# Two one-column values of each attention tile made on ScalarE instead of VectorE, expert loads issued one by one, and every slot rewritten

## The chip, the core and the metric

The kernel runs on one core of a Trainium2 chip. The metric is the device time of one execution in microseconds. A core has five engines that matter here: TensorE (PE in the profile, its weight loads PEld), VectorE (DVE), ScalarE (ACT), GpSimd (POOL) and SyncE (SP), which issues most of the loads and stores. Each engine takes its instructions in the order in which they are written; across engines, semaphores hold an instruction back until another one is done.

## What is computed

The input is 8 batches of 512 rows of 256 values, with a context of 1024 rows of 192 values for each batch. A layer normalisation, then a cross attention that keeps the 32 largest scores of each row, then a convolution over time done as a Fourier transform, a feed-forward layer, and at last a mixture of eight experts, of which each row goes to one, beside a shared one:

```python
Q = (x_text @ Wq).reshape(Bb, Tt, H, DH)                      # 4 heads of 32
scores = jnp.einsum('bthd,bghd->bhtg', Q, K) / np.sqrt(DH)
topv, topi = jax.lax.top_k(scores, K_TOP)                     # 32 of 1024
probs = jax.nn.softmax(topv, axis=-1)
attn = zeros.at[..., topi].set(probs); attn_mean = attn.mean(axis=1)
c_t = jnp.einsum('btg,bgd->btd', attn_mean, V)
# c_t scales and shifts the rows ahead of and behind the convolution s4d
x = x + jnp.tanh(g_xattn) * layernorm(xt + gelu(layernorm(xt) @ W1 + b1) @ W2 + b2)
x = x + jnp.tanh(g_ffn) * (shared(h) + expert[argmax(h @ gate_w)](h * score))
```

The same operation as before and after the change is asked for: the softmax over the 32 kept scores of each row and head.

## The kernel before

**Tiles and batches.** Attention works in 128 tiles, 16 to a batch: four groups of 128 rows, four heads each. Tile n's scores (128 x 1024) are made by TensorE in two of four PSUM banks (L1967, L1968). VectorE then finds the 32 largest of each row in four rounds: a maximum of eight (L1491 from PSUM, L1499 from SBUF) and a replacement that strikes these eight out (L1495, L1503), the replacement only after the first three rounds. ScalarE makes the exponential of all scores from PSUM, the sum of exponentials of the 32 kept ones, a ramp that tells kept scores from others (L1117), the logarithm of the reciprocal sum, and with it the exponential that turns the ramp into 0 or the reciprocal sum. GpSimd multiplies that by the exponentials and adds up the four heads (L776, L778, L780). TensorE turns the sum and multiplies it with the context (L1986, L1995).

**Two small values.** Each tile needs minus its scaled maximum, as the bias of the exponentials, and the reciprocal of its sum. Before, VectorE makes both in `limits()` (L1511 and L1514), counted by one semaphore, `v_limit`. The first must come behind the tile's first maximum, the second behind ScalarE's sum. ScalarE's `attention()` waits for the first ahead of its exponential of all scores and for the second ahead of the logarithm. Columns 0 to 3 of the tile's small buffer `sm` hold minus the scaled maximum, the sum, the reciprocal and its logarithm; there are three of these buffers, two each of `ee` and `tk`, the wide ones. A replacement of tile n writes `tk[n % 2]`, which GpSimd's product of tile n - 2 must have read.

**Behind attention.** For each batch: forward transform (L2211), spectrum, inverse transform (L2223), normalisations (moments, an ScalarE root, a GpSimd correction), a feed-forward layer with Gelu (L2247, L2257), the router, the shared expert (L2312, L2321). Rows are scattered to regions of DRAM by expert. From the fourth batch on 21 full tiles of 128 rows of one expert are worked off between the other work (`tiles()`, L2331 to L2351), each with its rows (L679) and its expert's weights (L684, L689) loaded by SP. In the last stage all eight experts' weights are loaded into the space that attention has left (`expert()`, L693 to L697), and the 18 remaining tiles run in a loop (L2370, L2380).

**What sets the order.** Every engine has a list of generators, one for each kind of work, that yield a number ahead of each piece: its slot. `weave` takes the piece with the smallest slot, then that generator's next, so a piece whose slot is smaller than what has gone before follows at once, and the numbers only set an order. Tile n's slots are counted from 8n. The tables of slots stand at the head of the file. `keep_warm` lets TensorE multiply a constant (L1945) a given number of times ahead of a piece; the FILL tables give the counts. ScalarE's functions come in tables; a change of table is an instruction of its own.

**SP's queue.** `late()` loads the inverse transform's table and the second weight of the feed-forward layer (L616, L617), `keys()` moves a batch's keys into place (L640, L642), `post()` reads x a second time (L662) and stores four result blocks (L667), `routed()` loads the experts.

Of the kernel before, what the change touches and what calls it, by code (L numbers as in the profile page):

```python
# [14 lines left out]
ALU = mybir.AluOpType  # L15
# [111 lines left out]
def tile_slot(j, table, step=0):  # L127
# [14 lines left out]
POOL_RESIDUAL = ((130.1, -4.1, -719.1, -97.8), (-203.7, 134.9, -261.3, -103.3))
POOL_OUT = ((-4044.4, -1439.6, -1614.3, -1706.4), (-1035.6, -458.3, -104, -271.7))
POOL_ROUTE = ((132.7, -16.2, -361.3), (135.4, 143.2, 144.9))
POOL_SH = ((238.9, -304.4, 243, 166.5), (152.6, 8.2, -1104.8, -2520.3))
POOL_PREP = (74, 75)
POOL_LOW = (105.1, 75.4, 76.7)
ACT_FILM_IN = ((43.7, -264, -187.1, -62.9), (-23.2, -497.2, 31.1, -313.4))
ACT_INV = ((69.3, -21.2), (48.4, -137.9))
ACT_FILM_OUT = ((72.4, -176, -155.8, -229), (51.5, -210.2, -467.8, 61.9))  # L150
ACT_ROOT = ((75.3, -138.8, 139.6), (71, -4004.6, 95.2))
ACT_NORM = ((84.6, 143.1), (-574.9, 50.3))
ACT_TURN = ((89.8, -324.7), (-4056.4, -177.3))
ACT_UP = ((99, 87.7, -389.9, 83.9, -76.5, -267.9, 106.2, -123.2), (-24, 84.5, -1154.9, -1053.5, 0.4, -343.5, -15.1, -1046.2))
ACT_DOWN = ((116.6, -45.3, -83, 121.2), (13.1, -263.3, 107.4, -198.8))
ACT_OUT = ((129.9, -538.2, 43.2, -140), (59.2, -943.2, -1370.1, -755.4))
ACT_TURN2 = ((147.5, -1744.3), (109.2, -588.1))
ACT_ROUTE = ((-3375.8, 83.1), (-1449.5, 127.6))
ACT_SILU = ((118.7, 155), (91.5, 140.1))
ACT_SH = ((166.5, -331.8, 168.6, 91), (145, -206.6, -505.3, -552.7))  # L160
DVE_SPECTRUM = ((115.4, -156.1, 116.8, -505.8), (54.3, -166.3, -118.6, -647.3))
DVE_MOMENTS = ((137.1, 171.7), (-368.7, 86.3))
DVE_ROUTE = ((177, 181.9), (51.2, -62))
ACT_PREP = (30, 35.9, -1091.9)
ACT_QUERY = (44.4, 21.7, 50.3)
ACT_CONTEXT = (26.7, 72)
ACT_KEY = (38.4, 74)
ACT_FINISH = ((20.6, -514.7, 28, 42), (34.8, 23.8, 43.8, 50), (29.1, -233.8, 44.8, 57.6), (19.5, -36.9, 31.7, 37.5))
POOL_SUM = (108.4, 104.3, 102.5, 68.5, 92.9, 86.6, 82, 74.3, 67.3, 59.7, 52.2, 24.3, 36.6, 28.7, 20.9, -8.4)
ACT_EXP = (34.5, 31.2, 36.7, -211.4, 29, 29.8, 25.2, 31.1, -302.9, 33.2, 34.4, 31.7, 34, 31, 37.7, 34)  # L170
ACT_SUM = (-5577.9, -2454.2, -13702.4, -367.4, -2349, -2050.3, -4001.9, -993.1, -582.7, -749.3, -321.1, -935.2, -8297.8,
          -1389.8, -2235, -2937.1)
ACT_GAP = (-3792, -696.7, -4814.2, -1077.2, -1503.7, -813.7, -1677.2, -1059.7, -4174.3, 34.4, -360.6, -410.7, -3110.4,
          -3466.1, -1110.4, -136)
ACT_CUT = (-4272, -335.4, -9847.4, -2245.8, -4171.1, -2117.7, -987.3, 37, 37, -976, 36.1, -5331.2, 36.5, -1921.3, -5870.9,
          -6698.4)
DVE_TOP = ((61.6, 62.3, 3.1, -30.7, -364.2, 68, -177.5), (68.2, -162.5, 73.2, -80.4, -286.6, 85.1, -418.3), (82, 89.6, -540.2,
# [18 lines left out]
PE_PREP = (-18, -17.9, -3.8, -3.8, -3.8, -3.2, 0.5, 0.6, 4.4)
POST_AT = ((1.4, 1.7, 2, 3.2, 12.6, 16, 16.3, 16.4, 18.2, 20.6, 21.2, 22.8, 23.2, 23.9, 33.3, 33.8, 35.5, 37, 38.2, 43.5,
# [4 lines left out]
SP_QUERY = (83.9, -1376.4, -528.1, -1221.3)  # L202
SP_KEYS = (159.4, -401.5, -433, 123.1)
SP_INPUT = (83.1, 133.9)
SP_POST = ((139.3, 140, -317.2, 88.8, -256.7), (75.3, 138.3, -308.4, -375, -253.9))
# [2225 lines left out]
```

## Time and profile before

| | us |
|---|---|
| median of three runs | 1727.35 |
| lowest and highest | 1720.44, 1732.33 |
| the profiled execution | 1728.4 |
| its span, first to last instruction | 1726.6 |

Busy shares of the span: TensorE 88%, VectorE 80%, GpSimd 67%, ScalarE 66%; 115 MB are moved. An engine's busy time counts no waiting. In rows of the profile, "L1499" is line 1499 of the kernel, names such as ZB or R are the large tensors from which the kernel cuts its buffers, and what stands in square brackets or behind the bar is the time that the engine was idle just before, with what ended it. The granted clock of TensorE over the execution is 0.952 of full.

### The profile page before, as it was taken

What the parts mean: (1) busy time and instruction counts of PE and PEld (TensorE: products, weight loads), DVE (VectorE), ACT (ScalarE), POOL (GpSimd) and SP (SyncE); (2) the same over time, 40 slices, a digit from 0 to 9 for tenths busy, and PEclk for the clock granted to TensorE, in tenths of its full rate; (3) what the DMA queues carried; (4) which work ended last, traced back from release to release, by engine and by line L of the source; (5) the groups of instructions that cost most, each with busy time, mean ns of one, the idle gap of its engine ahead of it and who ended that gap; (6) DMA issues with size and microseconds to landing.
All of it is one profiled execution on the core that took longest, in us unless ns stands there. A gap on an engine that the chain in (4) does not pass through costs nothing.

```text
span 1726.6 us, 22306 instructions
## 1 busy us (share of the span) xinstructions
PE 1516.2 (88%) x7299; PEld 1122.8 (65%) x7307; DVE 1383.0 (80%) x2241; ACT 1136.6 (66%) x2069; POOL 1152.6 (67%) x1267
## 2 busy tenths in 40 slices
PE   5887877798978897899999999999999999979996
PEld 3464555566646664667676767677767776747896
DVE  7798979997999899979898889889888998324421
ACT  3589955785688658765887678767886578122442
POOL 1498946757876787779768976898689858301322
PEclk8898999898989998899999999999999999989998
DMA  7200130002101210123323232323132212752431
GB/s 218 68 4 4 24 101 19 25 22 59 31 25 28 55 29 25 31 68 95 95 62 77 71 98 53 86 71 95 41 101 53 75 30 65 223 188 86 99 50 22
DMA packets 97223, 115.26 MB, mean 67 GB/s; under 512 B 17840, under 2 KB 74168, under 8 KB 96964
## 3 DMA queue, kind: packets, MB, share of 16 engines
q1 hardware_dynamic: 85348, 100.32, 19.9%
q0 software_dynamic: 11760, 13.52, 5.1%
q8 instruction: 58, 0.95, 0.2%
q14 instruction: 57, 0.47, 0.1%
HBM read 75.48 MB, written 19.58 MB: 55 GB/s over the span
## 4 chain that ended last, share of the span: by engine, by line
PE 35%; DVE 25%; ACT 16%; POOL 12%; issue 7%; DMA 2%; SPq 2%; POOLq 0%; DVEq 0%
DVE R L1499 7%; DVE ZB L1503 6%; PE PS L2370 4%; POOL ZB L778 3%; PE PS L2247 3%; PE PS L2223 3%; PE PS L1945 3%; DVE ZB L1495 3%; ACT ZB L1075 3%; PE PS L1995 3%; DVE R L1455 2%; ACT R L1081 2%; PE PS L2321 2%; DVE R L1491 2%; ACT ZB L1078 2%
## 5 line engine op out<-in xcount | busy, mean ns | idle before, releaser
L1499 DVE MAX8 R<-ZB 128x8 f32<-128x1024 f32 x384 | 470.9, 1226 | 10.3
L1503 DVE MATCH_REPLACE8 ZB<-R,ZB 128x1024 f32<-128x1024 f32 x256 | 309.4, 1209 | 0.0
L1945 PE MATMUL PS<-R 128*128 128x256 f32 x1048 | 279.6, 398 | 14.8 <-ACT R L1078 11.3
L778 POOL TENSOR_TENSOR ZB<-ZB 128x1024 f32<-128x1024 f32 x95 | 230.1, 2422 | 87.2 <-ACT ZB L1075 87.1
L1078 ACT ACTIVATE R<-PS 128x512 f32<-128x512 f32 (+6 forms) x404 | 172.6, 464 | 143.2 <-PE PS L2185 30.3
L1945 PEld LDWEIGHTS PS<-R 128*128 128x128 f32 x1048 | 199.3, 199 | 62.9 <-issue 17.7
L780 POOL TENSOR_TENSOR ZB<-ZB 128x1024 f32<-128x1024 f32 x95 | 224.2, 2360 | 7.4
L1491 DVE MAX8 R<-PS 128x8 f32<-128x1024 f32 x128 | 156.0, 1219 | 28.9 <-PE PS L1968 28.9
L1075 ACT ACTIVATE R<-R 128x32 f32<-128x32 f32 (+2 forms) x356 | 96.9, 273 | 100.1 <-DVE R L1511 29.9
L1495 DVE MATCH_REPLACE8 ZB<-R,PS 128x1024 f32<-128x1024 f32 x128 | 155.5, 1215 | 0.0
L1075 ACT ACTIVATE ZB<-ZB,R 128x1024 f32<-128x1024 f32 x128 | 147.1, 1149 | 4.2
L1075 ACT ACTIVATE ZB<-PS,R 128x1024 f32<-128x1024 f32 x128 | 142.0, 1109 | 3.3 <-DVE R L1511 2.1
L1117 ACT ACTIVATE ZB<-PS,R 128x1024 f32<-128x1024 f32 x128 | 141.3, 1104 | 0.0
L776 POOL TENSOR_TENSOR ZB<-ZB 128x1024 f32<-128x1024 f32 x32 | 77.2, 2413 | 74.9 <-ACT ZB L1075 74.9
L2312 PE MATMUL PS<-R 128*128 128x512 f32 x256 | 123.7, 618 | 0.0
L1995 PE MATMUL PS<-ZB 128*128 128x193 f32 x512 | 103.5, 361 | 21.4 <-ACT R L1078 9.2
L2247 PE MATMUL PS<-R 128*128 128x512 f32 x256 | 117.1, 601 | 2.4 <-ACT R L1078 1.1
L2257 PE MATMUL PS<-R 128*128 128x256 f32 x512 | 116.2, 379 | 1.7 <-ACT R L1342 1.7
L1995 PEld LDWEIGHTS PS<-ZB 128*128 128x128 f32 x512 | 95.9, 212 | 31.9 <-issue 17.9
L2257 PEld LDWEIGHTS PS<-R 128*128 128x128 f32 x512 | 95.6, 189 | 16.7 <-issue 1.7
L1039 POOL DMA_INDIRECT out<-R x21 | 34.0, 1617 | 104.8 <-ACT R L1078 92.1
L1967 PE MATMUL PS<-ZR 97*128 97x512 f32 x128 | 77.4, 605 | 25.2 <-ACT ZB L1117 16.2
(284 smaller groups left out, 3170.4 us busy)
## 6 DMA issues: line engine op xcount, KB each, us to landing
ZR<-ZR SPq DMA_DIRECT2D x96, 128.0 KB
ZB<-in_L_ffn_rt_gate SPq DMA_DIRECT2D x21, 512.0 KB, 4.1
ZB<-in_L_ffn_rt_up SPq DMA_DIRECT2D x21, 512.0 KB, 4.9
ZB<-in_L_ffn_rt_down SPq DMA_DIRECT2D x21, 512.0 KB, 6.1
R<-in_x SPq DMA_DIRECT2D x16, 512.0 KB, 4.2
ZB<-in_ctx SPq DMA_DIRECT2D x8, 768.0 KB, 4.9
R<-xs_d SPq DMA_DIRECT2D x39, 128.5 KB, 2.1
out<-R SPq DMA_DIRECT2D x32, 128.0 KB, 2.5
```

The lines of the kernel that those rows point to most:

```text
L778: pool.tensor_tensor(e, e, w, ALU.mult).then_inc(s.g_att, 1)
L780: pool.tensor_tensor(acc, acc, e, ALU.add).then_inc(s.g_att, 1)
L1075: return act.activation(*x, **k)
L1078: return act.activation(o, i, ACT.Copy, **k)
L1491: vec.max(ml[:, 0:8], sc_bank(n)).then_inc(s_tk[n % 2], 1)
L1495: vec.match_replace(w, ml[:, 0:8], sc_bank(n), NEG).then_inc(s_tk[n % 2], 1)
L1499: vec.max(ml[:, 8 * r:8 * r + 8], w).then_inc(s_tk[n % 2], 1)
L1503: vec.match_replace(w, ml[:, 8 * r:8 * r + 8], w, NEG).then_inc(s_tk[n % 2], 1)
L1945: pe.matmul(q_bank(*key)[:, 0:256], ident, warm, start=True, stop=True)
L1995: ins = pe.matmul(q_bank("finish", t, 2)[:, 0:CW], att[:, g, :], cb[b % 2][:, g, :], start=g == 0, stop=g == 7)
L2247: ins = pe.matmul(q_bank("post", b, UP + k), w1[:, c, k * 128:(k + 1) * 128], tr_post[:, c, :], start=c == 0, stop=c == 1)
L2257: ins = pe.matmul(q_bank("post", b, DOWN + i)[:, 0:256], big[:, k, i * 128:(i + 1) * 128], w2[:, k, :], start=k == 0, stop=k == 7 and b == ...
```

## The change

VectorE's generator `limits()` and its semaphore go. ScalarE makes minus the scaled maximum with a copy ahead of the exponential, and waits for that copy. It takes the logarithm of the sum itself, and a second copy changes its sign, which replaces the reciprocal; the exponential waits for it as before. The loads of experts 2 to 7, one piece before, become six pieces with slots of their own, with the same waits. All slot and filler tables have new numbers. The diff, cut to its core:

```diff
@@ SyncE, routed() @@
-                yield post_at(B - 1) + 12
-                on.wait_ge(s.v_tk0, 8 * PASS * B)
-                on.wait_ge(s.v_tk1, 8 * PASS * B)
-                on.wait_ge(s.v_last, 2)
-                on.wait_ge(*q_run("finish", 4 * B - 1, 3))
-                for e in range(2, E):
-                    expert(e)
-                yield post_at(B - 1) + 51
+                for k in range(6):
+                    yield post_at(B - 1) + SP_EXPERT[k]
+                    on.wait_ge(s.v_tk0, 8 * PASS * B)
+                    on.wait_ge(s.v_tk1, 8 * PASS * B)
+                    on.wait_ge(s.v_last, 2)
+                    on.wait_ge(*q_run("finish", 4 * B - 1, 3))
+                    expert(2 + k)
+                yield post_at(B - 1) + SP_EXPERT[6]
                 on.wait_ge(*q_run("post", B - 1, FILM_OUT + 3))
                 on.wait_ge(*q_run("post", B - 1, INV + 1))
                 expert(1)
-                yield post_at(B - 1) + 114
+                yield post_at(B - 1) + SP_EXPERT[7]
                 on.wait_ge(*q_run("tile", FULL - 1, T_DOWN))
                 expert(0)
@@ ScalarE, attention() @@
                     on.wait_ge(s_tk[n % 2], PASS * (n // 2) + 2)
-                    on.wait_ge(s.v_limit, 2 * n + 1)
                     on.wait_ge(s.g_att, added(n - 2))
+                    on.wait_ge(s.a_att, 5 * (n - 3) + 5)
+                    top = own.then_inc(copy(q[:, 0:1], ml[:, 0:1], scale=-SCALE))
+                    on.wait_ge(own.sem, top)
                     exp(e, sc_bank(n), ACT.Exp, bias=q[:, 0:1], scale=SCALE).then_inc(s.a_att, 1)
...
                     yield tile_at(n) + ACT_CUT[n % 16]
-                    on.wait_ge(s.v_limit, 2 * n + 2)
-                    exp(q[:, 3:4], q[:, 2:3], ACT.Ln).then_inc(s.a_att, 1)
+                    on.wait_ge(s.a_att, 5 * n + 2)
+                    log = own.then_inc(exp(q[:, 2:3], q[:, 1:2], ACT.Ln))
+                    on.wait_ge(own.sem, log)
+                    copy(q[:, 3:4], q[:, 2:3], scale=-1.0).then_inc(s.a_att, 1)
                     on.wait_ge(s.a_att, 5 * n + 4)
                     exp(w, w, ACT.Exp, bias=q[:, 3:4], scale=-STEEP).then_inc(s.a_att, 1)
@@ VectorE @@
-            def limits():
-                for n in range(16 * B):
-                    ml, q = mx[n % 3], sm[n % 3]
-                    yield tile_at(n) + DVE_LIMIT[n % 16][0]
-                    on.wait_ge(s_tk[n % 2], PASS * (n // 2) + 1)
-                    on.wait_ge(s.a_att, 5 * (n - 3) + 2)
-                    TS(q[:, 0:1], ml[:, 0:1], -SCALE, None, ALU.mult).then_inc(s.v_limit, 1)
-                    yield tile_at(n) + DVE_LIMIT[n % 16][1]
-                    on.wait_ge(s.a_att, 5 * n + 2)
-                    vec.reciprocal(q[:, 2:3], q[:, 1:2]).then_inc(s.v_limit, 1)
@@ tables @@
+SP_EXPERT = (165.6, 65.8, 77.2, -8.4, 121.4, 214.3, 99.9, 343.4)
-SP_LATE = (138, 255.9)
+SP_LATE = (231.4, 320.1)
-SP_KEYS = (159.4, -401.5, -433, 123.1)
+SP_KEYS = (211, -389, -469.1, 135)
-SP_POST = ((139.3, 140, -317.2, 88.8, -256.7), (75.3, 138.3, -308.4, -375, -253.9))
+SP_POST = ((205.4, 286.2, -283, -17.8, -229.6), (160.7, 248.2, -562.5, -595.2, -506.4))
...
```

Put in order by `weave`, SP's queue is the same as before but for these places: `late()` comes behind the keys of batch two and the third context instead of ahead of them; each batch's second reading of x comes ahead of the input of two batches on; and at the end the order

```
before: rows 17, weights 17, experts 2 to 7, rows 18, weights 18, rows 19, expert 1, second x, weights 19, rows 20, weights 20, expert 0, result rows
after:  rows 17, weights 17, rows 18, weights 18, rows 19, second x, experts 2 to 7, expert 1, weights 19, rows 20, weights 20, result rows, expert 0
```

(numbers are the full expert tiles').

## Rows read from the trace of the kernel before

**Rows 1.** Windows: stretch, us, PE, PEld, DVE, ACT, POOL, clock, DMA.

```profile
421.30:585.10 163.80, 140.28 (x564) 98.37 (x563) 152.27 (x239) 119.73 (x237) 126.30 (x133) 0.95 0.15 36
...
752.30:933.70 181.40, 173.74 (x823) 131.95 (x822) 156.95 (x244) 137.40 (x262) 140.88 (x172) 0.99 0.31 83
```

**Rows 2.** Groups by line, VectorE: shapes, count; busy us, mean ns; idle before.

```profile
L1514 DVE RECIPROCAL R<-R 128x1 f32<-128x1 f32 x128 | 19.5, 152 | 26.4 <-ACT R L1075 26.3
L1511 DVE TENSOR_SCALAR R<-R 128x1 f32<-128x1 f32 x128 | 18.1, 142 | 0.0
```

**Rows 3.** Timeline of VectorE, 533 to 545: start, length, instruction.

```profile
533.79 1.22 DVE L1491 MAX8 R<-PS 128x8 f32<-128x1024 f32 x1
...
535.12 1.21 DVE L1495 MATCH_REPLACE8 ZB<-R,PS 128x1024 f32<-128x1024 f32 x1
...
537.71 1.21 DVE L1503 MATCH_REPLACE8 ZB<-R,ZB 128x1024 f32<-128x1024 f32 x1
...
538.96 1.23 DVE L1499 MAX8 R<-ZB 128x8 f32<-128x1024 f32 x1
...
542.68 1.22 DVE L1491 MAX8 R<-PS 128x8 f32<-128x1024 f32 x1
...
544.07 1.21 DVE L1495 MATCH_REPLACE8 ZB<-R,PS 128x1024 f32<-128x1024 f32 x1
```

**Rows 4.** Timeline of ScalarE, 867 to 885.

```profile
867.26 0.20 ACT L1075 ACTIVATE R<-R 128x1 f32<-128x1 f32 x1
867.50 1.15 ACT L1075 ACTIVATE ZB<-ZB,R 128x1024 f32<-128x1024 f32 x1
...
884.70 0.20 ACT L1075 ACTIVATE R<-R 128x1 f32<-128x1 f32 x1 [3.63 <-DVE R L1511]
```

**Rows 5.** Groups by line, ScalarE, the small exponentials and logarithms.

```profile
L1075 ACT ACTIVATE R<-R 128x32 f32<-128x32 f32 (+2 forms) x356 | 96.9, 273 | 100.1 <-DVE R L1511 29.9 <-DVE R L1499 28.8 <-DVE R L1514 16.8
```

**Rows 6.** Timeline of all engines, 523 to 526.

```profile
523.04 2.35 POOL L776 TENSOR_TENSOR ZB<-ZB 128x1024 f32<-128x1024 f32 x1 [6.33 <-ACT ZB L1075]
...
525.27 0.16 DVE L1514 RECIPROCAL R<-R 128x1 f32<-128x1 f32 x1 [2.96 <-ACT R L1075]
...
525.50 1.21 DVE L1495 MATCH_REPLACE8 ZB<-R,PS 128x1024 f32<-128x1024 f32 x1
```

**Rows 7.** Chain of work that ended last, fifth batch: start, length, step.

```profile
833.60 1.11 ACT ZB L1075
...
910.04 1.15 ACT ZB L1075
```

**Rows 8.** Timeline of SP, VectorE and TensorE, end of batch one.

```profile
232.22 0.43 SPq L616 DMA_DIRECT2D R<-in_c_g  x1
...
239.86 1.23 DVE L1499 MAX8 R<-ZB 128x8 f32<-128x1024 f32 x1
...
246.43 0.77 PE L1967 MATMUL PS<-ZR 97*128 97x512 f32 x1 [7.54 <-issue]
...
247.66 1.23 DVE L1491 MAX8 R<-PS 128x8 f32<-128x1024 f32 x1 [6.58 <-PE PS L1968]
```

**Rows 9.** Windows, the gap at the end of batch one; last column GB/s.

```profile
233.20:246.40 13.20, 2.83 (x17) 1.95 (x15) 7.72 (x13) 5.13 (x9) 4.69 (x2) 0.87 0.97 268
```

**Rows 10.** Timeline of SP and TensorE in the last stage.

```profile
1482.90 0.44 SPq L693 DMA_DIRECT2D Z<-in_L_ffn_rt_gate  x1
...
1506.91 3.62 PE L2223 MATMUL PS<-R 128*128 128x256 f32 x16
...
1511.10 0.55 SPq L679 DMA_DIRECT2D R<-xs_d  x1
...
1519.76 0.47 PE L2331 MATMUL PS<-R 128*128 128x128 f32 x1 [9.23 <-DMA R<-xs_d]
...
1520.24 4.99 PE L2223 MATMUL PS<-R 128*128 128x256 f32 x16
...
1567.52 1.72 PE L2342 MATMUL PS<-R,ZB 128*128 128x128 f32 x14
```

More of the change, by code:

```diff
@@ L142 @@
[L142 to L168, printed above, removed]
@@ L248 @@
-FILL_TILE = ((0, 3, 1, 0), (0, 0, 0, 1), (6, 1, 4, 2), (0, 0, 1, 4), (0, 0, 2, 0), (0, 0, 0, 0), (0, 0, 0, 1), (0, 0, 0, 1),
-          (0, 0, 0, 2))
+POOL_FILM_IN = ((123.1, -574.3, 111.1, 95.8), (-309.3, -652, -402.7, 99.1))
+POOL_FOLD = ((-5415.1,), (-1378.7,))
+POOL_SPECTRUM = ((124.6, -334.2, 118.4, -166.7), (72.9, -141.4, -790.5, -646.9))
+POOL_INV = ((126, -50.9), (127, 121.3))
+POOL_FILM_OUT = ((50.4, -917.4, -564.3, -1178.8), (30.3, -115.2, -182.4, -588.7))
+POOL_ROOT = ((126.8, 132.3, 132.4), (41.9, 114.1, 65.5))
@@ new lines @@
+POOL_RESIDUAL = ((128.8, 25.3, -703.7, -32), (-203.7, 134.9, -261.3, -103.3))
+POOL_OUT = ((-4179.2, -1462.5, -1561.3, -1673.6), (-1035.6, -458.3, -104, -271.7))
+POOL_ROUTE = ((132.8, 17.7, -261.3), (135.4, 135.4, 64))
+POOL_SH = ((244.9, -313.6, 249.3, 230.8), (151.2, -32, -1036.9, -2662.5))
+POOL_PREP = (71.4, 73.3)
+POOL_LOW = (106, 73.4, 76.5)
+ACT_FILM_IN = ((46.6, -291.2, -74.9, -135), (-23.2, -497.2, 31.1, -313.4))
+ACT_INV = ((69.8, 32.1), (48.4, -137.9))
+ACT_FILM_OUT = ((73.2, -172.7, -179.2, -203.4), (52.8, -308.3, -505, 53.4))
@@ new lines @@
+ACT_ROOT = ((81.2, -187.8, 143), (73.1, -4011.1, 95.4))
+ACT_NORM = ((85.2, 146.6), (-574.9, 50.3))
+ACT_TURN = ((93.1, -383.1), (-3977.3, -177.3))
+ACT_UP = ((96.2, 93.4, -452.4, 76.2, -23.9, -146.7, 107.8, 2.9), (-169, 90.3, -1174.8, -963.7, -122.1, -544.1, -121.1,
+          -1102.1))
+ACT_DOWN = ((119.1, 23.2, -152.6, 124.1), (13.1, -263.3, 107.4, -198.8))
+ACT_OUT = ((128, -428.3, 84.5, -111.9), (59.2, -943.2, -1370.1, -755.4))
+ACT_TURN2 = ((147, -1801.1), (108.2, -588.1))
+ACT_ROUTE = ((-3518.3, 35.9), (-1361.1, 127.6))
@@ new lines @@
+ACT_SILU = ((133.8, 167), (69.8, 117.3))
+ACT_SH = ((170.7, -356.5, 172.1, -9.9), (144.4, -200.5, -572.7, -449.2))
+DVE_SPECTRUM = ((128.7, -119.3, 129.6, -538.6), (54.3, -166.3, -118.6, -647.3))
+DVE_MOMENTS = ((139.4, 180.6), (-368.7, 86.3))
+DVE_ROUTE = ((189.6, 197.2), (-102.8, -84.6))
+ACT_PREP = (30.1, 38.8, -1073.8)
+ACT_QUERY = (43.3, 27.8, 51.5)
+ACT_CONTEXT = (27.9, 71.4)
+ACT_KEY = (41.5, 73.9)
+ACT_FINISH = ((23.9, -542.2, 26.8, 43.5), (35.9, -9.5, 39.5, 54.1), (31.6, -261.6, 44.8, 65.4), (31.6, -43.8, 35.2, 40.1))
@@ new lines @@
+ACT_SHUP = ((156.6, 143.3, 167.5, 86.7), (112.6, -362.8, 119.9, 122.9))
+POOL_SHUP = ((132.9, -331.8, 99.8, -2030.3), (148.7, -461.3, -37.5, -2199.8))
+ACT_MOMENTS = (21.8, 26.8)
+PE_WEIGHT = (-72.1, -65.9, -45.9, -41, -1, -0.8)
+ACT_WEIGHT = (-97.6, 4.5, -3026.9, -450, -150.1)
+DVE_WEIGHT = (-9.2,)
+POOL_WEIGHT = (85.5,)
+DVE_RAY = (-36.4, -550.3, -82.6)
+ACT_RAY = (-3.3, -26.1, 0.5)
+PE_RAY = (-80, -75.8, -60.9)
+DVE_CHUNK = ((-3.6, 63.8), (94.3, 99.8), (118, 126), (130.8, 137.9), (139, 152), (153.5, 155.9), (158.6, 161.9), (165, 170.9))
@@ new lines @@
+POOL_CHUNK = ((43.4, -657.5, 104, -1158.7), (-677.7, -564.5, 123.3, -2079), (-436.1, -219.7, 124, -1184.2), (64.3, 40.3, 127,
+          -3149), (-580.6, -655.2, 127.6, -3303), (-285.4, -435.4, 102.8, 129.9), (-144.1, 128.7, 131.2, -1483.9), (-703.8,
+          -8.4, 131.5, -888.8))
+SP_CHUNK = (237.9, 275.9, 243.2, 225.5, 272.1, 306.5, 279.3, 267.2, -4097.2)
+SP_LATE = (231.4, 320.1)
+PE_END = (82.7, 87.5, 106.1, 110.9, 113.6, 118.8)
+ACT_END = (161.5, 164.4, 154.6, -942.5, -84, 155.3)
+DVE_END = (200.1, 208.2, 211.2, -35.7, 216.8, -1490.1)
@@ new lines @@
+DVE_CLOSE = (87.6, 107.8, 75, 74.3, 2.2, 25.8, 100.2, 110.6, -232.6, 92.8, -57, 75.9, 116.6, 99.3, 12.6, 69.1, 90.1, -230.4,
+          -188.7, 119.3, 125.3, -157)
+FILL_SCORES = (1, 0, 0, 0, 10, 0, 0, 0, 0, 0, 0, 0, 0, 0, 0, 5)
+FILL_FINISH = ((0, 0, 0, 2), (0, 0, 0, 0), (1, 0, 0, 0), (0, 0, 0, 0))
+FILL_PREP = (0, 0, 0, 0, 0, 0, 1, 2, 3)
+FILL_WEIGHT = (7, 0, 0, 2, 1, 5)
+FILL_RAY = (1, 9, 0)
+FILL_CHUNK = ((2, 0, 0, 0, 7, 0), (2, 0, 7, 1, 0, 0), (2, 0, 5, 0, 0, 0), (4, 3, 3, 0, 0, 0), (10, 5, 10, 1, 6, 0), (2, 4, 4,
+          0, 0, 7), (1, 0, 1, 3, 2, 0), (0, 1, 3, 1, 0, 1))
@@ L1931, in routed @@
                         vec.tensor_copy(yts[j % 3], PS[:, 3, 0:256]).then_inc(s.v_yt, 1)
-            weave(setup(), attention(0), attention(1), limits(), shares(), last_sum(), prep(), weights(), kernel_rows(), post(), close(), tiles(), routed())
+            weave(setup(), attention(0), attention(1), shares(), last_sum(), prep(), weights(), kernel_rows(), post(), close(), tiles(), routed())
         @block.tensor
```

110 lines of the change are left out of this document (37 added, 73 removed), and 20 rows, old and new, of tables (DVE_TOP, POST_AT).

## The prediction

> **What bounds the kernel now.** I read the busy time by stretch first, cut where every sixteenth attention tile starts (one "batch": 16 tiles) [rows 1]. Without expert tiles a batch takes 163.8 us and VectorE is busy for 152.3 of them; with expert tiles it takes 181.4, and TensorE is busy for 173.7, part of it filler products that the kernel issues while it has nothing to do. No engine is full. Then I read the chain of waits. In batches one to four it runs mostly through VectorE's maxima and replacements, in five to eight through TensorE, ScalarE and GpSimd in turn, and the expert batches hold a stretch of some 80 us (first and last step in [rows 7]) that is ScalarE's in large part. So the end is set by the order of dependent steps, and an instruction costs its length where it stands on that chain, and nothing elsewhere. Two waits on the chain are loads behind loads on SP's queue [rows 8, 10].
>
> **The change, part by part.** Attention tile n is 1024 scores a row. Before, VectorE made two one-column values per tile (minus the scaled maximum, and the reciprocal of the sum); now ScalarE makes both.
>
> *What VectorE loses.* 128 reciprocals of 152 ns and 128 scalings of 142 ns: 37.6 us of busy time [rows 2]. Little of it is path. From a maximum to the replacement behind it is 1.33 us without the pair (533.79 to 535.12) and 1.39 with it (542.68 to 544.07); from a replacement to the next maximum with the pair between them (537.71 to 538.96) the maximum starts 0.04 us after the replacement ends [rows 3]. The pair runs in the shadow of the long instruction in front of it: 0.00 to 0.06 us, a little more where it meets other small ones. The chain names such a pair some 22 times; at 0.06 to 0.08 that is 1.5 us. I take -1.5; the bounds are 0 and -37.6.
>
> The Trainium skill, "VectorE: DVE Perf Modes", section "The DRAIN you can't avoid", says otherwise: the next operation does not start before the pipe is empty, and one should minimise the number of operations. By that rule each of the 256 would be path at its full length. These rows do not show it.
>
> *The waits that go.* VectorE's reciprocal also waited for ScalarE's sum (for instance 2.96 us at 525.27). But the replacement behind it needs the buffer that GpSimd's product of two tiles before has to release, and that ended at 525.39, 0.11 us before the replacement started [rows 6]. Of 14 such waits (23.0 us together) nine have GpSimd's end within 0.2 us of the replacement, so they only change their name; the other five together could give 5 us, in batches where the chain is not on VectorE then. I take nothing. On ScalarE the logarithm waited for the reciprocal: 29.9 and 16.8, 46.7 us in all [rows 5] (the row names both of VectorE's lines, since one counter serves the two values). The regular case is tile 10 of each batch, 3.63 us at 884.70 [rows 4]. Soon after it ScalarE is idle again and waits for a maximum, so this too is absorbed. I take nothing.
>
> *What ScalarE gains.* Each tile has a scaling that the exponential must wait for, and a negation between the logarithm and the exponential of the weights. No row shows these two, but the logarithm is a one-column operation with the same kind of follower: 867.26 to 867.50, 0.24 us from start to start [rows 4]. So 0.48 us a tile, 61.4 us in all, where the 46.7 us of waiting went. On the chain I counted the places where it passes the start of a tile's exponential or the logarithm, leaving out those where it came back to VectorE through the reciprocal: 6, 2, 6, 5, 11, 11, 11 and 8 in the eight batches, 60 together (the fifth batch's are between the two rows of [rows 7]). 60 x 0.24 = +14.4 us. Bounds: 0 (all of it in gaps) and +61.4 (all on the path). I stay with the count, as the order of instructions on ScalarE hardly changes: read from the slots, it has as many changes of function table as before (124), and only some neighbours change places.
>
> *The load order at the end of batch one.* On SP the inverse transform's table and the second weight (1 MB each, issued at 232.22) stand ahead of the keys of batch two. TensorE then sits idle for 7.54 us until 246.43; VectorE had ended its last maximum at 241.09 and starts the next at 247.66 [rows 8]. With the new slots these two loads go behind the keys and behind the third context. 2 MB at the 268 GB/s that move in that gap [rows 9] are 7.8 us, and VectorE cannot start before 241.1, so at most 6.5 can be had. I take -5.6 and keep 0 and -6.5 as bounds. The table's first reader is the inverse transform of batch one's tail, well after the third context's load, so its being late costs nothing. The other swap on SP, each batch's second reading of x ahead of the input of two batches on, lets a wait be met earlier and costs nothing.
>
> *The expert loads.* Before, eighteen loads of 512 KB for six experts are issued in one go from 1482.90; the rows of expert tile 18 stand behind them and are issued at 1511.10. TensorE idles 9.23 us for them, until 1519.76, and then the second sixteen products of the inverse transform take 4.99 us where the sixteen ahead of the wait took 3.62 [rows 10]; I count the difference to the wait. In the new order the rows and weights of tile 18 and the rows of tile 19 go first, then the second reading of x, then all seven experts, then tile 19's weights. VectorE, which sat behind the second half of that transform, moves with it. So 9.23 + 1.37 = -10.6 us. What is late next: tile 19's weights wait behind 21 loads. These can start once tile 17 is written out, which I estimate at 1513; at the 28 us that eighteen took, the weights are issued by about 1545 and land by 1551 to 1555. They are needed at 1567.52 - 10.6 = 1557 [rows 10]. The cover is 2 to 6 us; gone, it costs one for one. Expert 0 goes behind the four result rows, which is a few us and far from its first reader. Bounds: 0 and -10.6.
>
> *Slots and fillers.* Everywhere else the slots give VectorE, TensorE and GpSimd nearly the same order; the exchanges (a score product past an expert product, a GpSimd scatter past a product) I price at 0, between -8 and +8. Fillers go from 524 to 563, most of the new ones ahead of batch two and in the last stage, where TensorE waits for others; they are in those 8 us.
>
> **Sum.** -1.5 + 14.4 - 5.6 - 10.6 = -3.3 on the profiled execution of 1728.4 (span 1726.6 and 1.8 around it): 1725.1. That execution is 1.05 above the median of three, so 1724.0 for the median.
>
> **The rivals.**
> *The additions are absorbed.* ScalarE has 46.7 us of waiting less, and its 0.48 us a tile may sink into that; then 14.4 falls to about 0 and exchanged neighbours may bring a little: 1727.35 - 1.5 - 16.2 = 1709.6, down to 1700. For it: ScalarE is busy only 119.7 of 163.8 us [rows 1]. Against it: in the expert batches the chain stays on ScalarE for many steps without a gap between them. A form of it is that VectorE's relief counts in full: in the four batches that VectorE leads, 64 x 0.294 = 18.8 us more, 1691. [rows 3] speaks against it. This is what the page named above makes of the change.
>
> *ScalarE becomes the bound, and it is slower.* Place: the stretch of each batch in which it runs without a gap, and the first batch, where it also makes the kernel values. If two thirds of the 128 tiles pay the 0.48 us on the path (+41) and the sums then come so late that VectorE's next tile waits, the time is 1727.35 + 41 - 1.5 - 16.2 = 1750.6. It decides from about 140 steps on the chain instead of 60. For it: GpSimd's products already wait for ScalarE's exponentials in most tiles. Against it: the count.
>
> *The expert loads only move their stall.* If tile 19's weights land 10 us late, the last stage gives its gain back: 1734. For it: the thin cover. Against it: the loads start no later than I estimate unless tile 17's scatter is slow.
>
> **How the numbers follow.** About 1% (17 us) is what a measurement of this kernel can tell from no change. The forecast, 1724 with a range of its own of 1712 to 1736: 0.55. Absorbed: 0.24, most of it under 1710. ScalarE the bound: 0.11. Stall moved: 0.10, inside 1%. The range that leaves out 2 in 10 is 1702 to 1742. Faster by over 1% (under 1710): 0.23; within 1%: 0.66; slower: 0.11.
>
> **What would show it.** In the profile after: no idle of TensorE for the rows of tile 18, and none of over 2 us ahead of the first score product of batch two; ScalarE busy about 256 x 0.2 us more; its waits for VectorE's one-column values gone; VectorE's replacements waiting longer for GpSimd's products; batches five to seven each 2 to 3 us longer, the first shorter by about 4. The forecast is wrong if the expert batches keep their 177 us or lose some (absorbed), if they grow by over 5 us (ScalarE the bound), or if TensorE waits for weights between the down product and tile 19.

## The result, and the profile after

| | us, median (runs) | against before |
|---|---|---|
| before | 1724.4 (10) | |
| changed | 1735.2 (10) | 1.0070, 95% interval 1.0054 to 1.0085 |

The changed kernel is 10.9 us slower by the medians; the forecast was 3.3 faster. It lies in the range and within 1%, but on the other side of no change. Its profiled execution (1733.1 us, span 1731.3) is the fastest of its ten. The windows of batches three, five and seven stand beside [rows 1]; columns as there.

```profile
410.80:579.20 168.40, 141.61 (x570) 99.56 (x569) 150.25 (x207) 125.47 (x270) 126.71 (x134) 0.95 0.15 35
...
752.80:937.90 185.10, 178.72 (x843) 136.04 (x842) 153.17 (x211) 144.47 (x297) 140.41 (x172) 0.99 0.29 81
...
1116.40:1298.90 182.50, 172.42 (x781) 130.07 (x780) 152.95 (x211) 139.93 (x289) 140.22 (x172) 0.96 0.27 73
```

Batch three went from 163.8 to 168.4, batch five from 181.4 to 185.1. In both, VectorE has 2 to 4 us less to do and ScalarE 6 to 7 more: the work moved as written, and the batches grew. The two one-column groups on ScalarE, by form (it had only the 128 logarithms before):

```profile
L1075 ACT ACTIVATE R<-R 128x1 f32<-128x1 f32 x257 | 50.9, 198 | 4.0
L1072 ACT ACTIVATE R<-R 128x1 f32<-128x1 f32 x128 | 25.2, 197 | 0.1
```

The 48.2 us of idle time ahead of the logarithms (29.9 and 16.8 for the two lines of [rows 5]) are 0.1 now. Both load gaps are gone as well. TensorE at the end of batch one and in the last stage (for [rows 8, 10]):

```profile
239.91 0.59 PE L1935 MATMUL PS<-R 128*128 128x256 f32 x2
240.16 0.59 PE L1957 MATMUL PS<-ZR 97*128 97x512 f32 x1
...
1518.98 0.27 PE L2322 MATMUL PS<-R 128*128 128x128 f32 x1
1519.09 7.08 PE L2213 MATMUL PS<-R 128*128 128x256 f32 x32
```

No idle time stands ahead of batch two's first score product (7.54 us before), and the inverse transform runs its thirty-two products without a break. What came instead is in VectorE's waits. First before, then after, both from 70 to 1455 us (engine, what waits, for what: us, times, longest):

```profile
DVE R L1514 <- ACT R L1075: 25.8, 20, 3.0
DVE ZB L1495 <- POOL ZB L776: 20.2, 5, 5.9
...
DVE ZB L1495 <- POOL ZB L778: 10.9, 13, 1.6
```

```profile
DVE ZB L1496 <- POOL ZB L773: 40.9, 12, 4.3
DVE ZB L1496 <- POOL ZB L775: 31.0, 32, 1.9
```

These rows belong to one ring of waits, called the ring below: a replacement on VectorE needs a buffer that GpSimd's product releases, the product needs ScalarE's exponentials, which need VectorE's maxima, and the reciprocal waited for ScalarE directly. The name changed as forecast ("they only change their name"), but the sum did not stay: 25.8 + 20.2 + 10.9 = 56.9 before, 40.9 + 31.0 = 71.9 after.

### The profile page after: what moved, and what is told of

Read it like the earlier page. It is cut to its first block and busy times, and to the rows that moved or that the text cites. A ratio compares the mean times of both kernels' runs of the same rounds, so it can differ in the third digit from the quotient of the medians.

```text
span 1731.3 us, 22633 instructions
## 1 busy us (share of the span) xinstructions
PE 1535.2 (89%) x7374; PEld 1143.6 (66%) x7385; DVE 1363.8 (79%) x1985; ACT 1180.0 (68%) x2325; POOL 1151.0 (66%) x1267
## 5 line engine op out<-in xcount | busy, mean ns | idle before, releaser
L1500 DVE MAX8 R<-ZB 128x8 f32<-128x1024 f32 x384 | 471.3, 1227 | 12.1
L1935 PE MATMUL PS<-R 128*128 128x256 f32 x1126 | 292.3, 394 | 19.0 <-ACT R L1075 14.8
L1075 ACT ACTIVATE R<-PS 128x512 f32<-128x512 f32 (+6 forms) x404 | 173.6, 465 | 153.1 <-PE PS L2175 33.1
L1935 PEld LDWEIGHTS PS<-R 128*128 128x128 f32 x1126 | 212.4, 198 | 67.0 <-ACT R L1075 17.9
L1985 PE MATMUL PS<-ZB 128*128 128x193 f32 x512 | 107.6, 371 | 21.6 <-ACT ZB L1075 10.6
L1985 PEld LDWEIGHTS PS<-ZB 128*128 128x128 f32 x512 | 100.0, 220 | 30.6 <-issue 16.2
L2247 PE MATMUL PS<-R 128*128 128x256 f32 x512 | 115.7, 378 | 0.0
L2247 PEld LDWEIGHTS PS<-R 128*128 128x128 f32 x512 | 96.2, 189 | 14.1 <-issue 0.4
```

The source lines that it names most:

```text
L1075: return act.activation(o, i, ACT.Copy, **k)
L1500: vec.max(ml[:, 8 * r:8 * r + 8], w).then_inc(s_tk[n % 2], 1)
L1935: pe.matmul(q_bank(*key)[:, 0:256], ident, warm, start=True, stop=True)
L1985: ins = pe.matmul(q_bank("finish", t, 2)[:, 0:CW], att[:, g, :], cb[b % 2][:, g, :], start=g == 0, stop=g == 7)
L2247: ins = pe.matmul(q_bank("post", b, DOWN + i)[:, 0:256], big[:, k, i * 128:(i + 1) * 128], w2[:, k, :], start=k == 0, stop=k == 7 and b == ...
```

## The experiments

Every kernel is timed against the kernel before on the same chip; the ratio is its time over that of before, and "us" is what the ratio adds or takes at 1725. "Depth" is the number of steps in a row on ScalarE that each tile has to wait for. Each trace is of one execution and can be some us off its kernel's median: e3_late's is the slowest of seven (1724.6, median 1712.6), e6_max's the fastest of seven (1726.5, median 1731.8). Together first:

| kernel | what it is | ratio (interval) | us |
|---|---|---|---|
| e1_move | before, both values on ScalarE | 1.0110 (1.0081, 1.0140) | +19.0 |
| e6_max | before, scaled maximum alone moved | 1.0050 (1.0032, 1.0069) | +8.6 |
| e7_log | before, negated logarithm alone moved | 1.0079 (1.0050, 1.0107) | +13.6 |
| e16_depth | before, two idle steps added on ScalarE | 1.0147 (1.0123, 1.0172) | +25.4 |
| e8_fill | e1_move and two more fillers a batch ahead of the turn | 1.0136 (1.0115, 1.0157) | +23.5 |
| e3_late | before, two 1 MB loads later | 0.9926 (0.9905, 0.9947) | -12.8 |
| e4_experts | before, expert loads later | 0.9941 (0.9918, 0.9964) | -10.2 |
| e5_loads | before, both load changes | 0.9868 (0.9844, 0.9892) | -22.8 |
| e9_both | e1_move and e5_loads | 1.0002 (0.9982, 1.0021) | +0.3 |
| changed | e9_both and all redone slots | 1.0070 (1.0054, 1.0085) | +12.1 |
| e2_slots | changed, values back on VectorE | 1.0272 (1.0246, 1.0298) | +46.9 |
| e12_back | the same, one pair placed later | 1.0044 (1.0028, 1.0060) | +7.6 |
| e13_pe | e9_both, TensorE's new slots, fillers | 1.0180 (1.0157, 1.0202) | +31.1 |
| e14_dvepool | e9_both, VectorE's and GpSimd's | 1.0107 (1.0087, 1.0127) | +18.5 |
| e15_act | e9_both, ScalarE's | 1.0156 (1.0129, 1.0184) | +26.9 |
| e10_act | changed, ScalarE's slots taken back | 1.0118 (1.0099, 1.0138) | +20.4 |
| e17_dvepool_old | changed, VectorE's and GpSimd's back | 1.0081 (1.0060, 1.0101) | +14.0 |
| e18_pe_old | changed, TensorE's slots, fillers back | 1.0152 (1.0132, 1.0173) | +26.2 |
| e11_fillers | changed, filler counts back | 1.0083 (1.0055, 1.0111) | +14.3 |

### The move alone, its halves, and its depth

The theory from the two traces: ScalarE's depth per tile is the price, and it is paid on the ring. The rival: the new slots are.

```diff
-                    on.wait_ge(s.v_limit, 2 * n + 1)
+                    top = own.then_inc(copy(q[:, 0:1], ml[:, 0:1], scale=-SCALE))
+                    on.wait_ge(own.sem, top)
-                    exp(q[:, 3:4], q[:, 2:3], ACT.Ln).then_inc(s.a_att, 1)
+                    log = own.then_inc(exp(q[:, 2:3], q[:, 1:2], ACT.Ln))
+                    on.wait_ge(own.sem, log)
+                    copy(q[:, 3:4], q[:, 2:3], scale=-1.0).then_inc(s.a_att, 1)
```

> The kernel before with the two one-column values made by ScalarE and nothing else: every slot, load and filler as before. My count of chain steps says +14.4 - 1.5 = +13 us against before, batches two to eight together +11 to +12, the first and last stretch unchanged. If the two values cost what ScalarE's depth per tile adds wherever GpSimd's product is waited for as well (the theory formed from the two traces: VectorE's wait for GpSimd grew from 18 places to 44), it is +18 to +25, with +2 to +5 in every batch from the third on. If the new slots are to blame for the batches that grew, this kernel is within 3 us of before.

Measured +19.0 (14 to 24), the middle of what the ring says and above the 13 of my count. ScalarE's timeline in tiles 46 and 47, e1_move first, then before (start, length, instruction):

```profile
556.40 0.19 ACT L1078 ACTIVATE R<-R 128x1 f32<-128x1 f32 x1
556.62 1.11 ACT L1075 ACTIVATE ZB<-PS,R 128x1024 f32<-128x1024 f32 x1
...
560.84 0.24 ACT L1075 ACTIVATE R<-R 128x1 f32<-128x1 f32 x1
561.10 0.20 ACT L1078 ACTIVATE R<-R 128x1 f32<-128x1 f32 x1
561.34 1.15 ACT L1075 ACTIVATE ZB<-ZB,R 128x1024 f32<-128x1024 f32 x1
...
565.39 1.15 ACT L1075 ACTIVATE ZB<-ZB,R 128x1024 f32<-128x1024 f32 x1
```

```profile
554.30 1.09 ACT L1075 ACTIVATE ZB<-PS,R 128x1024 f32<-128x1024 f32 x1
...
558.51 0.22 ACT L1075 ACTIVATE R<-R 128x1 f32<-128x1 f32 x1
558.76 1.15 ACT L1075 ACTIVATE ZB<-ZB,R 128x1024 f32<-128x1024 f32 x1
...
562.34 1.15 ACT L1075 ACTIVATE ZB<-ZB,R 128x1024 f32<-128x1024 f32 x1
```

The scaling costs 0.22 from its start to the exponential's, the negation 0.24. Over the stretch of two tiles (556.40 to 565.39 against 554.30 to 562.34) it is 8.99 against 8.04: 0.95 for four steps, 0.24 each. The size of a step was right.

```diff
 e6_max, in limits():
-                    TS(q[:, 0:1], ml[:, 0:1], -SCALE, None, ALU.mult).then_inc(s.v_limit, 1)
 e7_log, in limits():
-                    vec.reciprocal(q[:, 2:3], q[:, 1:2]).then_inc(s.v_limit, 1)
```

> The kernel before with only the scaled maximum moved to ScalarE (one step per tile, ahead of the tile's exponential; VectorE keeps the reciprocal). The whole move measured +19. If each of the two added ScalarE steps costs the same on the chain, this is about +9. If the price lies in the step ahead of the exponential, since that exponential is what GpSimd's product and through it VectorE's next replacement wait for, it is +14 to +19.

> The kernel before with only the reciprocal gone and the negated logarithm on ScalarE (VectorE keeps the scaled maximum). By equal steps about +9; if VectorE's 20 waits for ScalarE's sums (25.8 us) were path, the reciprocal's leaving gives something back here, and it is 0 to +5.

e6_max (VectorE keeps the reciprocal) gave +8.6, e7_log (VectorE keeps the scaling) +13.6, 22.2 together against 19.0 for both at once. The first meets equal steps. The second (8.6 to 18.5) is no cheaper, so the reciprocal's leaving gave nothing back that these times can show: its 25.8 us of waits were not path, or only a few us of them.

```diff
                     on.wait_ge(s.v_limit, 2 * n + 1)
+                    top = own.then_inc(copy(q[:, 4:5], q[:, 0:1]))
+                    on.wait_ge(own.sem, top)
...
                     on.wait_ge(s.a_att, 5 * n + 4)
+                    log = own.then_inc(copy(q[:, 4:5], q[:, 3:4]))
+                    on.wait_ge(own.sem, log)
```

> The kernel before with both values left on VectorE and two one-column copies added on ScalarE in each tile, whose results nobody reads but for which the exponential and the weights' exponential wait. If the depth of ScalarE is the price of the move, this is at e1_move's +19 or a little above (VectorE keeps its pair, at most +2). If the move cost by what VectorE and GpSimd do differently, the copies alone cost clearly less, under +10.

The two copies change nothing that is computed, and VectorE keeps its pair: +25.4 (21 to 30), where 19 to 21 was expected if depth is the price and under 10 if it isn't. So two more steps on ScalarE are enough for the whole price, and what VectorE loses in e1_move (256 instructions, and the reciprocal's waits) is worth 25.4 - 19.0 = 6.4 us, with about 7 either way, so not told from nothing. VectorE's waits on the ring in e16_depth, same columns and stretch:

```profile
DVE R L1518 <- ACT R L1075: 40.5, 37, 3.7
...
DVE ZB L1499 <- POOL ZB L776: 21.6, 5, 5.7
...
DVE ZB L1499 <- POOL ZB L778: 15.2, 24, 1.6
```

77.3 us against 56.9 before: 20.4 of the 25.4 stand here. In e1_move it is 49.7 + 22.6 = 72.3, 15.4 of its 19.0. By these rows most of the price stands on the ring.

### TensorE's clock behind the turn

Tile 14 of batches three and four grew by 2.4 and 4.3 us in e1_move, of five to eight by 1.1. TensorE there in batch three, e1_move, then before:

```profile
571.12 1.53 PE L2228 MATMUL PS<-R 128*128 128x128 f32 x8 [3.25 <-ACT R L1081]
572.44 1.91 PE L1938 MATMUL PS<-R 128*128 128x256 f32 x4
574.14 2.28 PE L2264 MATMUL PS<-R 128*128 128x8 f32 x16
```

```profile
568.33 1.10 PE L2235 MATMUL PS<-R 128*128 128x128 f32 x8 [2.00 <-ACT R L1081]
569.26 1.03 PE L1945 MATMUL PS<-R 128*128 128x256 f32 x4
570.26 1.92 PE L2271 MATMUL PS<-R 128*128 128x8 f32 x16
```

ScalarE is about 1 us late, TensorE idles 3.25 instead of 2.00, and then four filler products (two fillers; the trace has two products for each) take 1.91 instead of 1.03. The windows right behind the idle time, e1_move, then before, have the granted clock in the column behind the engines:

```profile
571.10:577.00 5.90, 5.88 (x30) 5.27 (x31) 2.05 (x6) 1.56 (x4) 3.74 (x3) 0.71 0.16 35
```

```profile
568.30:573.50 5.20, 5.17 (x32) 3.97 (x32) 3.71 (x12) 2.19 (x5) 3.99 (x4) 1.00 0.07 14
```

0.71 against 1.00: part of the stretch was at 1.2 GHz instead of 2.4. The Trainium skill, "TensorE: Matmul & The Clock Gate", Part 1, says that idleness puts the clock down and activity brings it back; the rows agree. The test was to fill the gap with work, two more fillers:

```diff
-FILL_POST = ((0, 0, 0, 1, 0, 0, 0, 0, 0, 0, 0, 0, 0, 0, 0, 1, 2, 0, 0, 0, 0, 0, 0, 0, 0, 0, 0, 0, 1, 0, 2, 0, 0, 0, 0, 2, 0,
+FILL_POST = ((0, 0, 0, 1, 0, 0, 0, 0, 0, 0, 0, 0, 0, 0, 0, 1, 2, 0, 0, 0, 0, 0, 0, 0, 0, 0, 0, 0, 3, 0, 2, 0, 0, 0, 0, 2, 0,
```

> The kernel before with both values on ScalarE, as in e1_move, and two more filler products ahead of the second turn in batches one to seven, so that TensorE's idle time there is as long as before (3.3 us became 2.0). In e1_move the sixteen gate products behind that gap took 2.3 and 3.4 us instead of 1.9 and 2.2, at a granted clock that had fallen to half, and tile 14 of batches three and four grew by 2.4 and 4.3 us where those of five to seven grew by 1.1. If the clock is the cause, tile 14 grows by about 1.1 in all of them and the time is 4 to 6 us under e1_move, +13 to +15 against before. If the gap is only longer by what ScalarE is late, the fillers change nothing: +19.

Measured +23.5, no better than e1_move. TensorE in batch three of e8_fill:

```profile
572.37 1.46 PE L1938 MATMUL PS<-R 128*128 128x256 f32 x6
576.02 1.35 PE L2228 MATMUL PS<-R 128*128 128x128 f32 x8 [2.20 <-ACT R L1081]
577.16 1.92 PE L1938 MATMUL PS<-R 128*128 128x256 f32 x4
```

The idle time is back at 2.20, yet the four filler products take 1.92 (granted clock 0.59 from 576 to 580). The clock fell all the same, so shortening this one gap did not keep it up. Batch four says the same of the length of the gap; first before, then e1_move:

```profile
734.15 1.65 PE L2235 MATMUL PS<-R 128*128 128x128 f32 x8 [2.98 <-ACT R L1081]
735.60 1.91 PE L1945 MATMUL PS<-R 128*128 128x256 f32 x4
```

```profile
741.24 1.09 PE L2228 MATMUL PS<-R 128*128 128x128 f32 x8 [2.87 <-ACT R L1081]
742.17 1.79 PE L1938 MATMUL PS<-R 128*128 128x256 f32 x4
```

Behind nearly equal gaps the eight products took 1.65 in the one and 1.09 in the other, and behind both the filler products were slow. The clock falls at this turn in the kernel before too, so it isn't something that the move alone brings. What it costs is seen from tile 14 of batch two: 20.5 us at a granted clock of 0.67 in the trace of before, 15.5 at 0.89 in that of e5_loads, which has the same order there. In batch four of e8_fill the gap was 1.30, the clock stayed up and tile 14 was 0.4 shorter than in before; in batch three it was 6.1 longer. So e8_fill did not take the clock out of the comparison; it shows only that these fillers don't make the kernel faster. From this comes a caution: with one and the same order of the attention tiles, batches two to four took 504.7 us in the trace of before, 501.4 in e4_experts, 502.0 in e5_loads and 504.8 in e3_late, and single ones differ by up to 6 (batch two 173.6 and 167.2). Batches five to eight took 696.9, 696.7, 696.7 and 699.0. The growth of single batches among two to four can't be read from two traces.

The sum over these three batches can be read from ten, and tile 14 can be taken out of it. With both steps on ScalarE (e1_move, e8_fill, e9_both, e16_depth) batches two to four took 516.6 to 518.6 us; without them (before, e3_late, e4_experts, e5_loads) 501.4 to 504.8; with one, e6_max took 503.1 and e7_log 516.7. Tile 14 of the three batches is 3.3 to 5.2 us of the growth in the kernels with both steps, 7.4 in e7_log and -5.6 in e6_max, where the four filler products took 1.03 us at all three turns. The other tiles grew by 6.7 to 9.6 with both steps, by 4.0 and 4.6 with one, and by -1.8 to 0.9 with none. So outside tile 14 the two steps cost alike and add in these traces, and the difference between e6_max and e7_log in these batches stands in tile 14, with a granted clock of 0.88 to 0.91 over it in the one and 0.66 to 0.85 in the other.

### The loads

```diff
-SP_LATE = (138, 255.9)
+SP_LATE = (138, 262)
```

> The kernel before with one slot on SP changed: the two 1 MB loads go behind the keys of batch two and the third context. Forecast: TensorE's 7.5 us idle at 239 to 246 shrinks and the end comes 5.6 us earlier (at most 6.5). Rival: the loads are late for the inverse transform of batch one's tail and give back what was won, 0.

-12.8 (-16.4 to -9.1): more than forecast. Its trace shows the 6.7 us in batch one's last tile that were to be had, and nothing else of that size. But that execution is 12 us above the kernel's median and only 3.8 below the profiled one of before, so it can't show where the other 6 us are. e5_loads, whose trace also has the 6.7, is 12.6 under e4_experts by the ratios: the size repeats, its source stays open.

```diff
+SP_EXPERT = (76, 76, 76, 76, 76, 76, 76, 114)
...
-                yield post_at(B - 1) + 12
+                for k in range(6):
+                    yield post_at(B - 1) + SP_EXPERT[k]
```

> The kernel before with the seven expert loads behind the loads of tile 18 and the rows of tile 19. Forecast: -10.6 us, the 9.2 us idle of TensorE at 1511 gone and 1.4 more behind it. What the changed kernel's last stage showed is -7.3: if the difference to -10.6 is a stall moved to tile 19's weights, this kernel shows TensorE waiting for weights for about 3 us behind tile 18.

-10.2 (-14.1 to -6.2), forecast -10.6; the last stage of its trace is 12.9 us shorter, and TensorE waits 0.8 us for weights in it (0.8 also in e5_loads), not 3. Nothing was moved to tile 19's weights.

e5_loads has both edits.

> The kernel before with both changes of the load order (the two 1 MB loads behind batch two's keys and the third context; the seven expert loads behind tile 18's loads, tile 19's rows and the second reading of x), the two values still on VectorE. The two alone measured -12.8 and -10.2 us. If they add, about -21 (1704); by my forecast's terms -16.2 (1709).

-22.8 (-26.9 to -18.6), median 1701.0: the two add. This kernel beats both.

### The redone slots

Its edit is that of e1_move, e3_late and e4_experts together.

> The kernel before with both values on ScalarE and both changes of the load order; every other slot and filler stays that of before. If the two parts add: 1725 + 19 - 24 = 1720, and the changed kernel's 1735 then holds some 15 us that are neither the move nor the loads but the redone slots. If the parts don't add (the chain on ScalarE eats what the loads free), it is at the changed kernel's 1735.

+0.3 (-3.1 to +3.6). The move and the loads together are at the kernel before, 19.0 - 22.8 = -3.8 by their sum. So the redone slots and fillers hold 0.0068 of the ratio, 11.7 us; with both intervals, 7.4 to 16.0.

```diff
 e2_slots, in the changed kernel's attention() on VectorE:
                     vec.max(ml[:, 0:8], sc_bank(n)).then_inc(s_tk[n % 2], 1)
+                    limits(n, 0)
 e12_back, the table of which pair stands behind which instruction:
-(10, 0): [('rec', -1), ('neg', 0)]
+(10, 3): [('rec', -1), ('neg', 0)]
```

> The changed kernel with the two values back on VectorE, each behind the same VectorE instruction as in the kernel before; slots, load order, expert loads and fillers stay the changed ones. If moving the values cost what the changed kernel lost, this gives -15 us against before (-8 at the first batches, -7 in the last stage, batches three to eight as before), so it is faster than both. If the slots are to blame, batches three to eight stay 10 to 20 us longer than before and the time is near or above that of before.

> As e2_slots (the changed kernel with both values back on VectorE), but tile 9's reciprocal and tile 10's scaling stand three VectorE instructions later. In e2_slots that pair stalled VectorE by 6 us in each batch, since ScalarE's new order makes tile 9's sum late. Without that stall: 1770 - 8 x 6 = 1722; if redone slots cost 15 by themselves and the move nothing more, 1715 to 1720.

e2_slots measured +46.9. Its waits on VectorE from 70 to 1455 us say why: a pair stands in VectorE's order where ScalarE's new order makes the sum late (two gelu pieces go ahead of tile 9's exponential).

```profile
DVE R L1495 <- ACT R L1072: 78.1, 23, 8.8
```

It is no measure of the slots. With that pair three instructions later (e12_back) it is +7.6, about 1733, where 1715 to 1720 was expected; other places for the pairs weren't tried. The values on VectorE and the loads alone were -22.8 with before's slots; with the new ones +7.6. The new slots cost 30 us with the values on VectorE and 12 with them on ScalarE: they suit the move better, and don't pay it back.

The next three replace whole tables of slots in e9_both, one engine's at a time; of ScalarE's, for instance:

```diff
-ACT_UP = ((99, 87.7, -389.9, 83.9, -76.5, -267.9, 106.2, -123.2), (-24, 84.5, -1154.9, -1053.5, 0.4, -343.5, -15.1, -1046.2))
+ACT_UP = ((96.2, 93.4, -452.4, 76.2, -23.9, -146.7, 107.8, 2.9), (-169, 90.3, -1174.8, -963.7, -122.1, -544.1, -121.1,
+          -1102.1))
```

> e9_both with TensorE's slots and fillers of the changed kernel. Among the exchanged orders is a score product (tiles 9, 13, 3 of each batch) that now stands on the other side of other products; if these hold the 11 us between e9_both and the changed kernel, this is +8 to +14 against before. If not, 0.

> e9_both with the slots of VectorE and GpSimd of the changed kernel. Tile 7 of each batch became 5 to 8 us longer and tile 8 as much shorter in the changed kernel: the first maximum of tile 8 stands behind the last of tile 7 and GpSimd's products of tiles 7 and 8 elsewhere. If that exchange holds the 11 us, this is +8 to +14; if it only moves a boundary, within 3 us of e9_both.

> e9_both with ScalarE's slots of the changed kernel. Going back to the old ScalarE slots in the changed kernel cost 8 us (e10_act), so by themselves they may help: -8 to 0 against e9_both. If they only fit the other engines' new slots, they cost here: +2 us a batch at tiles 9 to 11, about +15.

Against e9_both, TensorE's new slots and fillers cost 31 us, ScalarE's 27, VectorE's with GpSimd's 18: each more than all together. The expectations had 14 at most for e13_pe and e14_dvepool; that of e15_act named this case, at about +15. SyncE's slots, which still differ between e9_both and the changed kernel (each batch's second reading of x, expert 0), were tried in no run by themselves. The four that follow put the old tables of one engine back into the changed kernel.

> The changed kernel with all slots of ScalarE taken from the kernel before (gelu pieces six and seven and the last query piece stand behind tile 9's exponential again). In the changed kernel tiles 9 to 11 of every batch grew by 2 to 2.9 us, in the move alone by 1. If ScalarE's new order is the cause, this is 8 to 15 us faster than the changed kernel, about 1722 to 1727. If not, 1735.

> The changed kernel with the filler counts of the kernel before (524 instead of 563). If the added fillers stand in TensorE's way where it is wanted, this is faster by up to 39 x 0.25 = 10 us. If they keep the clock up, it is slower by some us. If they sit in idle time, no difference beyond 3 us.

> The changed kernel with VectorE's and GpSimd's slots of the kernel before. If the exchange at tiles 7 and 8 is what makes the changed kernel's batch five to seven and its last stage (3.7 us longer than in e9_both) slow, this is 5 to 10 us faster than the changed kernel, 1725 to 1730. If the slots fit each other only as a set, it is slower, 1740 to 1755.

> The changed kernel with TensorE's slots and fillers of the kernel before. If TensorE's new order holds the 11 us (alone on e9_both it cost 31), this is at e9_both's 0 to +5 against before. If the slots only fit as a set, it is slower than the changed kernel, 1740 to 1765.

Taken out of the changed kernel, ScalarE's and TensorE's cost 8 and 14 us more; the fillers alone and VectorE's with GpSimd's change it by 2, inside the intervals (the expectation of e17_dvepool_old had 5 to 10 faster, or slower, at 1740 to 1755). That 2 for the fillers may be two effects: in the trace of e11_fillers batch one is 15.0 us longer than in the changed kernel, and batches five to eight 6.5 shorter. The expectation of e10_act (8 to 15 faster) was wrong: the gelu exchange is right where the others are new. None of the four engines holds the 11.7 us by itself; their slots work as a set. A part of what the set does is seen in VectorE's waits over batches five to eight, e9_both from 754.6 to 1459.5, then the changed kernel from 752.8 to 1461.3:

```profile
DVE ZB L1500 <- POOL ZB L777: 36.1, 8, 6.3
DVE ZB L1500 <- POOL ZB L779: 13.0, 15, 1.6
DVE R L1654 <- PE PS L2265: 12.7, 4, 3.4
DVE R L1496 <- PE PS L1962: 10.2, 5, 3.2
DVE R L1890 <- PE PS L2336: 8.1, 4, 4.1
```

```profile
DVE ZB L1496 <- POOL ZB L773: 27.3, 8, 4.3
DVE R L1492 <- PE PS L1958: 17.1, 8, 4.6
DVE ZB L1496 <- POOL ZB L775: 16.3, 16, 1.9
DVE R L1886 <- PE PS L2332: 12.8, 4, 5.7
DVE R L1510 <- PE PS L1985: 8.2, 7, 1.9
DVE R L1650 <- PE PS L2261: 7.1, 4, 1.8
```

On the ring and at the gate VectorE waits 61.8 us in the one and 50.7 in the other; for score, share and expert products 18.5 (0.2 of it for the share, a row not shown) and 38.1. Here the ring is the waits for GpSimd, and the gate the router's product (L2265 and L2261). The new order takes 5.5 us from the ring and 5.6 from the gate and adds 20 for TensorE's other products; VectorE's busy time is some 6 lower, and the four batches took 704.9 and 708.5. The last stage grew as well, 266.3 to 270.0: in the windows around its gate, e9_both, then changed, the clock is lower and the stretch 3.2 us longer.

```profile
1584.80:1605.60 20.80, 20.80 (x70) 11.57 (x70) 13.34 (x45) 6.28 (x10) 9.49 (x12) 0.92 0.46 151
```

```profile
1587.30:1611.30 24.00, 23.41 (x66) 13.24 (x66) 14.49 (x47) 6.28 (x10) 9.36 (x13) 0.79 0.41 136
```

These are 3.6 and 3.7 us; batches one to four are 1.1 shorter in the changed kernel (684.9 and 686.0), and the two traces differ by 5.5 us in all. e9_both's profiled execution is 3.0 above its median and the changed kernel's 2.1 below, so about half of the 11.7 us stands in no row, and why this order is slower is shown only in part.

## Why the prediction was wrong

**Slots and fillers at 0 with bounds of 8.** This is the step that failed: 11.7 us (7.4 to 16.0) where I had 0, and by its middle outside the bounds. I compared orders and found "nearly the same"; some exchange in each batch was left, and the exchanges of TensorE, of ScalarE, or of VectorE and GpSimd alone cost 18 to 31 us.

**What ScalarE gains, +14.4.** The mechanism was right, the size wrong: 25.4. A step is 0.24 us, as taken; at that size it stands about 106 times (88 to 124) on what sets the end, not 60. The count gave 13 steps (3.1 us) to batches two to four, where the chain of waits names VectorE. e1_move lost 14 us there by its trace (518.6 against 504.7; 9.6 of it outside tile 14) and 6.4 in five to eight (703.3 against 696.9), where I had 41 steps and 9.8. My reading is that the chain names one path, and where VectorE's and the ring's are nearly equal in length, a step on the one that isn't named costs too; no run shows their lengths directly. The rival "ScalarE becomes the bound" needed 140 steps and stays a rival.

**VectorE's relief and the waits that go, -1.5 and 0.** 6.4 +- 7 for both; [rows 3] held, and of the 37.6 us of busy time and the 23.0 of waits no more than some 13 together can have been path. The rule of the Trainium skill, "VectorE: DVE Perf Modes", section "The DRAIN you can't avoid", by which I had each of the 256 as path, is not borne out: 25 ns each (0 to 52) instead of 147. I had left out a sentence of that section: "A next op that is not held starts earlier". The trace has such a start: the reciprocal between the rows at 537.71 and 538.96 of [rows 3] starts at 538.84, 0.08 us before the replacement ahead of it ends.

**The loads.** The experts -10.6: measured -10.2. The two 1 MB loads -5.6 with -6.5 as bound: -12.8; 6.7 are where I had them, the other 6 stay open. The rival of a moved stall is not borne out: TensorE waits for no weights in the changed kernel's last stage.

**The sum.** Without the slots I had -3.3, and e9_both measured +0.3 +- 3.3. But its terms were +12.9 and -16.2, and they measured +19.0 and -22.8: two errors of 6 us that cancelled, which is luck. The list of what would show it was met (both stalls gone, ScalarE's waits for the two values gone, replacements waiting for GpSimd), except for the batches: batches five to seven were to grow by 2 to 3 us each and grew by 3.7, 1.2 and 5.3, and that alone would not have told the slots from the steps.

## What to carry to other kernels

Where two rings of waits are nearly equal, a step added to either can cost in more rounds than those in which the chain names it: here 106 of 256, against 60 named. Take the count of the chain as the low side, and the full length in every round as the high side. A change that brings its own redone order is two changes; the order can't be priced at nothing because few neighbours changed places, and here its parts, put in one at a time, said nothing of the whole. The part that was worth most (1.3%) was the cheapest: large loads whose readers come late, moved behind small ones that are wanted now.

## What the hardware showed

A one-column instruction on ScalarE takes 0.20 us, and one that waits for it starts 0.22 to 0.24 us after it did, among instructions of 1.1 us. The Trainium skill, "ScalarE: Activation LUTs", section "What ACT_TABLE_LOAD costs", gives 186 ns and 0.83 ns per element for one with immediate scale and bias, which is 187 ns for one column; the trace has 198 for the copies, 6% more. On VectorE 256 small ones between long ones, with the waits that went with them, were worth 25 ns each (0 to 52). TensorE's clock fell to half behind an idle time of 2.20 us in e8_fill and stayed up behind 2.37 in e6_max, so the length of one gap does not tell. Single batches of one order of work differ by up to 6 us between executions, and 5 of them are one tile with the clock at 0.67 or at 0.89.
